# A four-block float32 network on one core: attention walked by chunks of queries, its output projection laid between the units, the second unit's maxima begun early, the last unit halved, and the value products in one group of 512 columns

## The reference, cut to what matters

```python
x = x + context @ Wo + bo                                # the rotary blocks
y = xn + (sigmoid(context @ Wg + bg) * context) @ Wout   # gated blocks, then a layer norm
```

## Time and profile before

| | us |
|---|---|
| median of 3 runs | 4048.62 (4042.51 to 4051.37) |
| time of the profiled execution | 4049.78 |
| its span | 4047.9 |
| TensorE, VectorE, ScalarE, GpSimd busy | 3594.8, 3088.4, 2272.1, 138.7 |
| the four attentions (first maximum to last L1893) | 829.9 to 1513.4, 1636 to 2318.5, 2587.2 to 3086.7, 3146 to 3829.4 |

### The profile page before, as it was taken

The page is one execution under the profiler, slowest core; times in us unless marked ns, Lnnn a source line. Parts: engine busy times, 40 slices in busy tenths (PEclk is TensorE's granted clock), DMA queues, the critical chain, the costliest instruction groups (busy, mean ns, idle before and its releaser), DMA issues.

```text
span 4047.9 us, 71976 instructions
## 1 busy us (share of the span) xinstructions
PE 3594.8 (89%) x29276; PEld 1462.3 (36%) x29276; DVE 3088.4 (76%) x6440; ACT 2272.1 (56%) x2630; POOL 138.7 (3%) x371
## 2 busy tenths in 40 slices
PE   5889889779999996799999987599997899999886
PEld 3755756412222223122222263233333122222362
DVE  5255545589999955899999547796875899999547
ACT  2222232228888882388888821157475388888821
POOL 0000000110000000000000000200000000000000
PEclk8889889869999997699999989699998699999988
DMA  0010510120000002200000000400001200000000
GB/s 29 2 50 1 119 38 1 35 86 2 2 2 2 2 2 57 86 2 2 2 2 2 23 1 0 115 2 2 2 2 41 75 2 2 2 2 2 23 1 11
DMA packets 32731, 84.57 MB, mean 21 GB/s; under 512 B 10096, under 2 KB 25232, under 8 KB 26000
## 3 DMA queue, kind: packets, MB, share of 16 engines
q1 hardware_dynamic: 32256, 78.17, 7.2%
q10 hardware_dynamic: 144, 1.79, 0.1%
HBM read 65.24 MB, written 14.70 MB: 20 GB/s over the span
## 4 chain that ended last, share of the span: by engine, by line
DVE 46%; PE 45%; ACT 4%; issue 3%; DMA 2%; SPq 1%; POOL 0%; ACTq 0%; DVEq 0%; POOLq 0%
DVE pm L1874 37%; PE ps L1815 9%; PE ps L1780 6%; PE ps L1800 4%; PE ps L949 3%; PE ps L952 3%; PE ps L2099 3%; PE ps L2075 3%; PE ps L1028 3%; ACT arena L1840 1%; PE ps L1477 1%; PE ps L1212 1%; PE ps L748 1%; DVE XN L293 1%; DVE stat L283 1%
## 5 line engine op out<-in xcount | busy, mean ns | idle before, releaser
L1874 DVE TENSOR_REDUCE pm<-ps 128x1 f32<-128x512 f32 (+2 forms) x3712 | 2214.5, 668 | 140.4 <-PE ps L1780 75.7
L1840 ACT ACTIVATE arena<-ps 128x1024 f32<-128x1024 f32 (+3 forms) x1856 | 1851.8, 1001 | 510.8 <-PE ps L1800 357.9
L1780 PE MATMUL ps<-arena 64*128 64x512 bf16 (+2 forms) x3712 | 1298.5, 396 | 29.1 <-DVE pm L1874 15.4
L1815 PE MATMUL ps<-arena,VA 128*16 128x256 f32 (+1 forms) x14592 | 1138.5, 384 | 40.4 <-ACT EV L1860 22.9
L1800 PE MATMUL ps<-arena 64*128 64x512 bf16 (+1 forms) x3712 | 1043.7, 379 | 21.5 <-DMA arena<-m_dram 20.7
L1780 PEld LDWEIGHTS ps<-arena 64*128 64x128 bf16 x3712 | 330.5, 93 | 1081.6 <-DVE pm L1874 894.9
L1815 PEld LDWEIGHTS ps<-arena,VA 128*16 128x16 f32 x14592 | 240.5, 94 | 511.0 <-ACT arena L1840 404.0
L1800 PEld LDWEIGHTS ps<-arena 64*128 64x128 bf16 x3712 | 195.7, 94 | 122.8 <-issue 78.6
L968 ACT ACTIVATE EV<-ps 128x512 f32<-128x512 f32 x128 | 76.3, 597 | 203.0 <-PE ps L949 203.0
L980 DVE TENSOR_TENSOR arena<-EV,ps 128x512 f32<-128x512 f32 x128 | 87.9, 687 | 124.8 <-PE ps L952 120.3
L949 PE MATMUL ps<-XNT,arena 128*128 128x512 f32 x304 | 160.7, 611 | 2.3 <-DVE arena L1255 1.5
(11 more groups left out here) (270 smaller groups left out, 2680.3 us busy)
## 6 DMA issues: line engine op xcount, KB each, us to landing
arena<-parts_dram SPq DMA_DIRECT2D x192, 128.0 KB, 2.9
parts_dram<-parts SPq DMA_DIRECT2D x32, 384.0 KB, 2.9
arena<-k_dram SPq DMA_DIRECT2D x20, 528.0 KB, 11.4
arena<-in_pad SPq DMA_DIRECT2D x16, 512.0 KB, 8.0
parts<-k_dram SPq DMA_DIRECT2D x8, 528.0 KB, 6.6
arena<-in_w SPq DMA_DIRECT2D x4, 1024.0 KB, 6.2
early<-in_late SPq DMA_DIRECT2D x1, 2184.5 KB, 8.9
VA<-k_dram SPq DMA_DIRECT2D x4, 528.0 KB, 7.7
```

What stands on the lines that cost most here:

```text
L1780: ins = e.matmul(bank[:, 0:w], QR[half(par), q, 2 * g + pp, qt * P:(qt + 1) * P], KT[half(par), kc, 2 * g + pp, 0:w], start=True, stop=not ...
L1815: ins = e.matmul(c.bank(4)[32 * hh:32 * hh + VW, a:b], c.VA[:, j, GH * g + hh, :], self.PB[:, (first + hh) % self.PBS, a:b], start=j == 0 ...
L1840: e.activation(self.PB[:, s:s + 2, offs[0]:CH], c.bank(t % 4, 2).rearrange("p (a t) -> p a t", a=2)[:, :, offs[0]:CH], ACT.Exp, scale=self ...
L1874: e.tensor_reduce(c.pm[:, u % 2, at, kc:kc + 1], self.slot_bank(slot)[:, 0:w], AX, ALU.max).then_inc(self.emptied_v.sem, 1)
```

## The change

The order of the units is now chunk by chunk, all four head groups of a chunk of queries in succession; the causal block takes the chunks in the order 0, 3, 2, 1. The last unit is cut into two units of one pair of heads each; its maxima, rows, values and output are done by halves. Fourteen maxima of the second unit are laid before the first scores, four of them ahead of the first unit's "rows". The value products are issued once per key tile, on 512 columns. When all heads of a chunk are there, new steps follow three steps apart, through the same three slots: "turn" (TensorE transposes the chunk, ScalarE copies), for the gated blocks "gate" (one float32 product of 512 columns, sigmoid with the bias by ScalarE, product with the context by GpSimd), and "project" (products with the weights, sum by VectorE). The bias of the other two blocks is added to the input by GpSimd at the stage's start. The stages `ProjectOut` and the first half of `GatedTail` fall away. The diff, cut to its core:

```diff
 class HeadsPlan:
-    LEAD = 9
-    def __init__(self, causal):
-        self.units = [(g, NC - 1 - k if g % 2 else k) for g in range(NG) for k in range(NC)]
+    LEAD, EARLY, AHEAD = 9, 4, 14
+    SCALAR = ("rows", "turn", "gate")
+    def __init__(self, causal, behind):
+        self.order = (0, 3, 2, 1) if causal else (0, 1, 2, 3)
+        self.units = [(g, k, (0, 1)) for k in self.order for g in range(NG)]
+        g, k, _ = self.units.pop()
+        self.units += [(g, k, (0,)), (g, k, (1,))]
...
+        if what == "out":
+            g, k, pairs = self.units[where[0]]
+            if g == NG - 1 and pairs[-1] == 1:
+                self.later.append([3, (self.behind[0], (k,), None)])
+        elif what in self.behind[:-1]:
+            self.later.append([3, (self.behind[self.behind.index(what) + 1], where, None)])
...
     def lay_out(self):
+        pending, reached, queued, total, clock = self.maxima(1), 1, [], 0, 0
+        queued.append((starts[1] - self.LEAD, len(pending)))
+        for n in range(min(self.AHEAD, len(pending) - 1)):
+            if n == self.EARLY:
+                self.tick(True)
+            self.run(pending.pop(0))
+            total += 1
...
-                    if waiting:
-                        self.values(*waiting[0], pp)
+                    if waiting and n_pair == len(pairs) - 1:
+                        self.values(*waiting[0])
...
 class Heads(Stage):  # tensor
             elif what == "values":
-                _, u, j, first, last, part = step
-                a, b = max(plan.tile_off[first], part * CH // 2), (part + 1) * CH // 2
-                e.wait_ge(*self.exped[plan.exp_of[first + 3]])
-                for hh in range(GH if a < b else 0):
-                    ins = e.matmul(c.bank(4)[32 * hh:32 * hh + VW, a:b], c.VA[:, j, GH * g + hh, :],
-                                   self.PB[:, (first + hh) % self.PBS, a:b], start=j == 0 and part == 0, stop=last,
-                                   tile_position=(0, 32 * hh), skip_group_check=True)
+                _, u, j, first, last = step
+                n_heads = 2 * len(pairs)
+                off = plan.tile_off[first]
+                e.wait_ge(*self.exped[plan.exp_of[first + n_heads - 1]])
+                for n in range(n_heads):
+                    hh = 2 * pairs[0] + n
+                    ins = e.matmul(c.bank(4)[32 * hh:32 * hh + VW, off:CH], c.VA[:, j, GH * g + hh, :],
+                                   self.PB[:, (first + n) % self.PBS, off:CH], start=j == 0, stop=last,
+                                   tile_position=(0, 32 * hh))
...
+class Project:
+    KINDS = ("turn", "project")
+    def gpsimd_first(self, e):
+        for k in range(NC):
+            if k:
+                e.wait_ge(*self.biased[k - 1])
+            e.tensor_tensor(self.xs(k), self.xs(k), bc(self.bias, TPC), ALU.add).then_inc(self.biased.sem, 1)
+    def turn(self, e, heads, k, bank):
+        e.wait_ge(*heads.ready(k))
+        for t in range(TPC):
+            ins = e.transpose(bank[:, t * P:(t + 1) * P], c.CTX[:, TPC * k + t, :], c.IDF[:, :])
+    def tensor(self, e, heads, what, k, bank):
+        e.wait_ge(*heads.emptied(heads.plan.slot_of["turn", k]))
+        for t in range(TPC):
+            ins = e.matmul(bank[:, t * P:(t + 1) * P], self.chunk(k)[:, t * P:(t + 1) * P], self.weights, start=True,
+                           stop=True)
+    def scalar(self, e, heads, what, k, bank):
+        return e.activation(self.chunk(k), bank, ACT.Copy)
+    def vector(self, e, heads, what, k, bank):
+        e.wait_ge(*self.biased[k])
+        return e.tensor_tensor(self.xs(k), tiles(bank), self.xs(k), ALU.add)
+class Gate(Project):
+    KINDS = ("turn", "gate", "project")
+    def gpsimd(self, e, heads, what, k):
+        if what == "gate":
+            e.wait_ge(*heads.emptied(heads.plan.slot_of["gate", k]))
+            e.tensor_tensor(self.sg(k), self.sg(k), self.chunk(k), ALU.mult).then_inc(self.gated.sem, 1)
+    def tensor(self, e, heads, what, k, bank):
+        if what == "gate":
+            e.wait_ge(*heads.emptied(heads.plan.slot_of["turn", k]))
+            return e.matmul(bank, self.gate, self.chunk(k), start=True, stop=True)
+    def scalar(self, e, heads, what, k, bank):
+        return e.activation(self.sg(k), bank, ACT.Sigmoid, bias=self.bias)
+    def vector(self, e, heads, what, k, bank):
+        return e.tensor_tensor(c.CTX[:, TPC * k:TPC * k + TPC, :], tiles(bank), c.XN[:, TPC * k:TPC * k + TPC, :], ALU.add)
...
-        then(Heads, False)
-        then(ProjectOut, chip.ep("wo2"), chip.ep("bo2"))
+        then(Heads, False, Project(chip, chip.ep("wo2"), chip.ep("bo2")))
...
-        then(Heads, False)
+        then(Heads, False, Gate(chip, chip.lp("mgate"), chip.lp("mgateb"), chip.lp("mout")))
         then(GatedTail)
```

More of the change, by code:

```diff
@@ L1628, in score_pair, with values @@
         self.tile_off += [off, off]
-        self.steps += [("scores", u, j, pp, first), ("exp", first, 2, self.exps)]
-        self.exp_of += [self.exps] * 2
-        self.exps += 1
-    def values(self, u, j, first, last, half):
-        self.steps.append(("values", u, j, first, last, half))
-        if last and half:
-            self.last_tile[u] = first + 3
+        self.steps += [("scores", u, j, pp, first), ("exp", first)]
+        self.exp_of += [first // 2] * 2
+    def values(self, u, j, first, last):
+        self.steps.append(("values", u, j, first, last))
+        self.value_of += [self.n_values] * (2 * len(self.units[u][2]))
+        self.n_values += 1
+        if last:
+            self.last_value[u] = self.n_values - 1
             self.steps.append(("empty", u))
-            self.later.append([4, ("out", u)])
+            self.later.append([4, ("out", (u,), None)])
     def lay_out(self):
@@ L1720, in gpsimd @@
         s = self.split
-        for u in range(len(self.plan.units)):
+        self.behind.gpsimd_first(e)
+        for step in self.plan.steps:
+            if step[0] in self.behind.KINDS:
+                self.behind.gpsimd(e, self, step[0], step[1])
+            if step[0] != "finish":
+                continue
+            u = step[1]
             k = u % 2
@@ L1768, in tensor @@
             what = step[0]
-            if what in ("max", "rows", "out") and step[-1] > 2:
+            if what in ("max", "rows", "out") + self.behind.KINDS and step[-1] > 2:
                 e.wait_ge(*self.emptied(step[-1] - 3))
@@ L2037, in tensor @@
         self.fence(e)
-        self.turn.tensor(e)
-        self.gate.tensor(e)
-        self.turn_gated.tensor(e, lambda i: e.wait_ge(*self.gated[i // TPC]))
-        self.product.tensor(e)
         for k in range(NC):
```

270 lines of the change are left out of this document (130 added, 140 removed).

## The result

The changed kernel takes 4137.58 us (median of 4 runs, 4135.33 to 4140.39) where the kernel before takes 4049.99 us in the same session (4 runs, 4042.51 to 4060.23): ratio 1.0215, 95% interval 1.0191 to 1.0239, slower by 88 us.

What follows compares the result with a forecast made beforehand. VectorE was taken to set the pace of three attentions, TensorE mostly that of the causal one. First block +19, gated blocks +23 each, causal -12: +53 us on 4049.8, so 4103 us, range 3975 to 4135.

Steps and rivals of the forecast that it cites:

- case A: Whole kernel: the three slots let the merged values show; 4075 to 4130 us, chance 0.55, the forecast itself.
- the four units of chunk 0: Causal block: four such units in succession have little work to hide VectorE's 64 maxima of the next chunk; +8 us.
- the bursts that fall away: Causal block: under the new order no more bursts of maxima come later; -20 us.
- Values in one group: Blocks without the mask: one 512-column group at 0.97 us makes VectorE wait; unit 40.8 us instead of 39.42, +19 us.
- The closed path: Three-slot ring, reduction to product to values to product to reduction: 2.44 us against VectorE's 2.39 for four reductions.
- Early maxima: Start of each unmasked block: 14 maxima, 8.4 us of reductions, move into VectorE's idle time; -8 us.
- Last unit halved: End of attention in unmasked blocks: a two-head value group still costs 0.97 us, steps take 1.29 us; +9 us.
- Projection inside: Three projection chunks between the units of an unmasked block: +5 us in the first block, +11 us in gated ones.
- The ends: Behind each attention only the last chunk's projection is left: -6 us in ungated blocks, -8 us in gated ones.
- The causal block: Masked attention, TensorE mostly setting the pace: all terms sum to -12 us with the end's -6, between -45 and +15.
- Rival D: Table loads, gate product and GpSimd hold exps back in full, or TensorE falls to 1.2 GHz: 4140 us, chance 0.10.
- Rival B: Slots still hide the values and a group of two heads costs half: 3970 us, chance 0.22.

Runs made afterwards that it cites:

- the run over 384 columns: Kernel after with each maximum over at most 384 of its columns and exp of a thousandth of the scores, used for time only: 3988.09 us.
- the two runs with two groups: Kernel after with two value groups of 256, whole last unit, old causal order: 4033.89 us; the same with all four projection chunks behind the last unit: 4014.66 us.
- the mixed run: Kernel after with two value groups outside the causal block, whole last units, old causal order, all projection chunks behind the last unit: 4005.34 us.

## Why the prediction was right in direction and short in size

The forecast was +53 us; the spans differ by +88.1, and 4137.58 us is 2.6 above the prediction's range of 3975 to 4135 (and above the 4130 of its own case A). The step that failed is the causal block: in its sum I had put the order by chunks at -12 us (+8 for the four units of chunk 0, -20 for the bursts that fall away) and the clock at nothing, and the runs show +17.3 for the order, with TensorE at 1.2 GHz for 79 us of the block instead of 34. It makes 17 of the 35 us; the rest is smaller sizes, the value group's above all. Point by point, as the prediction had them:

**Values in one group.** Right in mechanism. The closed path is there, 2.47 us for the predicted 2.44, and the run over 384 columns shows that it, not VectorE and not TensorE, sets the step. Half of the 0.03 us is the price of the group, 0.985 us where I took 0.97; the rest is spread over the other links. Sixteen steps make 0.5 us of it, and the output and rows steps give 0.3 back: they cost 0.35 us a unit (1.64 less 16 x 0.08) where I had 0.65. So the unit (41.05) is 0.25 above my 40.8, partly by two errors that cancel, and 13.6 units make 3.4 us per block.

**Early maxima.** -8 predicted; 6.5 to 7.8 us by the run without them. Right.

**Last unit halved.** +9 predicted, for the last 73 steps against those of the kernel before: 94.8 us for 85.8. The timelines have 94.2 (from the joined maximum at 1449.2 to 1543.4) for 85.5 there, +8.7. The step of 1.29 us came out to the digit. Right, although my sum counts only 72 of the 73 steps. The 10.1 to 10.2 us of the run with a whole last unit compare with something else: with a whole last unit and one value group the same steps take 84.1 us, 1.4 less than in the kernel before.

**Projection inside.** +5 and +11 predicted, 4.0 and 11.1 to 11.8 measured by the two runs with two groups; in the kernel after the units with a projection inside are 1.97 and 3.30 us longer than the others, 5.9 and 9.9 for three. Within the gate's 11 the table loads are some 0.7 us a chunk where I had 0.6. Right.

**The ends.** -6, -8, -6, -8, together -28; measured -6.5, -5.7, -4.6, -4.8, together -21.6. In the other kernels with the same ends the stretches behind the gated blocks are 5 to 8 us shorter than before, so these terms are off by at most 3 us each. The timelines behind the second attention show why, ScalarE and VectorE of the kernel after:

```profile
2377.87 1.28 ACT L2027 ACT_TABLE_LOAD   x1
2380.08 0.69 ACT L2027 ACTIVATE parts<-ps,early 128x512 f32<-128x512 f32 x1 [0.93 <-PE ps L2017]
2384.33 0.69 DVE L2031 TENSOR_TENSOR CTX<-ps,XN 128x512 f32<-128x512 f32 x1 [7.89 <-PE ps L2020]
...
2389.41 1.28 ACT L2334 ACT_TABLE_LOAD   x1 [8.64 <-DVE mv L2220]
```

From the last division to the end of the last chunk's sum it is 8.6 us (7.9 of them VectorE's wait at 2384.33) where I had 6.6, and the load for the square root, which the kernel before did beside other work at 2328.97, now stands in the open behind the statistics (2389.41). I had asked what is late next for the exps inside the attention, and not for the table at its end.

**The causal block.** -6 within the attention predicted, +11.3 measured; this is the largest miss, 17 us of 35, and the step that failed. In the sum I had +8 for "four units of chunk 0 in succession" and -20 for "no more bursts of maxima later", -12 for the order by chunks together; the run with the old order makes it +17.3. The other terms (narrow steps, rows, outputs, turns) were too dear by about as much as the rest of that gap. What I missed was the clock. Under the new order TensorE stays at its lower level of 1.2 GHz for most of 80 us (0.59; in the first 84 us from the first scores before it was 0.88), and in the causal block TensorE is what sets the pace. That the order made the 17.3 us is shown by the run with the old one. That much of it is the clock is argued from the windows and the table; no run shows how much.

Summed up from the measured parts, the first gated block is +21.4 merge, +10.1 halves, -7.8 early, +11.1 inside: +34.8, and +34.4 was found; the second +20.6 +10.2 -6.6 +11.8 = +36.0 for +34.0; the rotary block +20.3 +10.2 -7.0 +4.0 = +27.5 for +29.4. The parts add up to within 2 us, so nothing large is left unnamed there. In the causal block they don't add: 17.3 + 3.4 - 6.5 + 2.4 = +16.6 without the merge, +11.3 found, and the merge measured +6.2, -4.9 and -20.3 in three surroundings. Only with the -4.9 of the mixed run does the sum come near (+11.7), and nothing but the result speaks for that choice.

Rival D named 4140 us, very near the time found, but that is luck and not its way: loads in full, the gate and a fallen clock in the blocks without the mask have next to no part in it. Only its clause on TensorE at 1.2 GHz has something to it, in the causal block. Rival B is refuted on both its legs: the slots don't hide the values, and a group of two heads costs 0.97 us, not half.

## What to carry to other kernels

When a ring of buffers ties two engines, add up the closed path (here reduction, product, values, product) before making one of its links longer: a group of instructions that is cheaper in total can still be dearer, because it is one piece. Cut such work into pieces that fit between two releases, and place each piece where its input has had time. And before moving work under a full engine, count what it costs there: here 29 us inside for 7 at the ends.

## What had not been expected of the hardware

- A float32 value group on 16 weight columns and 512 columns costs TensorE 0.97 us for two strips of the array and 0.98 for four: leaving two of the strips out gives almost nothing. Groups of 448, 256 and 64 columns took 0.88, 0.56 and 0.24 us, so each has about 0.13 us around its columns.
- One group of 448 and one of 64 cost TensorE the same 1.12 us as two of 256, and the kernel 168 us more, through the wait for exp.
- A switch of ScalarE's table between exps, twice 1.28 us in its rows, cost the unit around it some 0.7 us for both.
- In the first 80 us from the causal block's first scores the mean clock was 0.50 to 0.59 in the order by chunks and 0.76 to 0.90 in the other, for products of the same kinds; with two groups of values it stayed at 1.2 GHz for 108 us while TensorE was busy 105 of them.
